# Where ScalarE's squares and VectorE's y1, E and V stand beside the y2 normalization

## The reference

```
q = x + x@Wq.T + bq ; k1, k2, v1, v2 likewise, 16 heads of 8
S1 = k1'v1/n ; S2 = k2'v2/n ; S12 = S1*S2        (8x8 per head)
out = q@S1*v2mean*g1 + rowsum(S12)*g2 + q@S2*v1mean*g3 + q@S12*g4
attn = layernorm(out)*ln_g + ln_b, then @ Wo.T + bo
x1  = layernorm(x + attn)
y2  = x1 + relu(x1@w1 + b1)@w2 + b2
y3  = layernorm(y2)*gamma + beta + x1
out = layernorm(y3)
```

## Time and profile before

| | |
|---|---|
| median of 3 runs | 218.47 us (216.88 to 219.51) |
| profiled execution, own time | 216.88 us |
| its span, first to last instruction | 215.1 us |
| PE busy | 195.6 us (91%) |
| DVE busy | 163.5 us (76%) |
| ACT busy | 127.5 us (59%) |
| POOL busy | 134.2 us (62%) |
| PE share of the chain that ended last | 54% |
| DVE, ACT shares of it | 18%, 13% |

### The profile page before, as it was taken

One profiled execution on the slowest core, in us unless ns is written; L12 is line 12 of the kernel. 1 busy time (PEld: TensorE's weight loads), 2 busy tenths in 40 slices (PEclk: granted clock), 3 DMA queues, 4 the chain that ended last, 5 costly groups with the idle time before them and its releaser, 6 DMA issues.

```text
span 215.1 us, 4255 instructions
## 1 busy us (share of the span) xinstructions
PE 195.6 (91%) x1380; PEld 177.9 (83%) x1380; DVE 163.5 (76%) x477; ACT 127.5 (59%) x383; POOL 134.2 (62%) x173
## 2 busy tenths in 40 slices
PE   7879999999998999899989999899989999899930
PEld 7768998997997889787979999798979998888630
DVE  0155845989868987989688886898697878896895
ACT  3122448455559585766576566947575557867571
POOL 8324650465896569675966489755967397776230
PEclk9999999999999999999999999999999999999995
DMA  5999700000010100110010001010011001011012
GB/s 157 103 292 287 188 0 5 2 0 5 0 49 0 52 2 3 49 50 0 0 52 34 16 3 49 0 53 0 0 52 52 0 0 52 0 50 49 2 50 98
DMA packets 12145, 9.98 MB, mean 46 GB/s; under 512 B 642, under 2 KB 9995, under 8 KB 12123
## 3 DMA queue, kind: packets, MB, share of 16 engines
q1 hardware_dynamic: 11082, 8.53, 12.8%
q0 software_dynamic: 320, 0.85, 2.6%
q10 hardware_dynamic: 720, 0.33, 0.6%
HBM read 5.51 MB, written 4.19 MB: 45 GB/s over the span
## 4 chain that ended last, share of the span: by engine, by line
PE 54%; DVE 18%; ACT 13%; issue 8%; DMA 3%; SPq 2%; DVEq 0%; ACTq 0%
PE down_ps L890 17%; PE up_ps L890 14%; PE prep_ps L890 12%; PE z_ps L890 7%; DVE st L689 5%; ACT res L571 5%; DMA vec_rows<-in_L_ffn_b 3%; PE turn_ps L1010 3%; DVE y2n L694 3%; DVE x1T_lo L826 3%; ACT hT L588 2%; ACT z_sq L549 2%; ACT x1T_hi L638 2%; DVE z_ps L788 2%; PE turn_ps L983 2%
## 5 line engine op out<-in xcount | busy, mean ns | idle before, releaser
L890 PE MATMUL down_ps<-w_sb,hT 128*128 128x128 f32 x496 | 61.1, 277 | 0.1
L890 PEld LDWEIGHTS down_ps<-w_sb,hT 128*128 128x128 f32 x496 | 58.4, 192 | 1.2 <-DVE y2n L694 0.4
L588 ACT ACTIVATE hT<-up_ps,cols 128x512 f32<-128x512 f32 x64 | 41.6, 682 | 3.7 <-PE up_ps L890 3.5
L503 POOL TENSOR_TENSOR x1b<-x,b_rows 128x512 f32<-128x512 f32 x16 | 20.6, 1287 | 19.1 <-DVE x L694 19.1
L890 PE MATMUL up_ps<-x1T_hi,w_hi 128*128 128x512 f32 x64 | 26.5, 414 | 4.1 <-ACT hT L588 4.1
L477 POOL TENSOR_TENSOR y2g<-y2n,gamma_rows 128x512 f32<-128x512 f32 x14 | 17.9, 1279 | 13.4 <-DVE y2n L694 13.4
L571 ACT ACTIVATE res<-y,nb,rstd 128x128 f32<-128x128 f32 x60 | 24.6, 483 | 2.1 <-POOL nb L465 2.1
L890 PE MATMUL up_ps<-x1T_lo,w_hi 128*128 128x512 f32 x64 | 25.5, 398 | 0.0
L890 PE MATMUL up_ps<-x1T_hi,w_lo 128*128 128x512 f32 x64 | 25.2, 395 | 0.0
L549 ACT ACTIVATE z_sq<-z_ps 128x128 f32<-128x128 f32 x64 | 16.9, 272 | 12.3 <-PE z_ps L890 12.3
L694 DVE TENSOR_SCALAR x<-z_ps,st,rstd 128x128 f32<-128x128 f32 x64 | 21.9, 404 | 0.6
(11 more groups left out here) (144 smaller groups left out, 426.1 us busy)
## 6 DMA issues: line engine op xcount, KB each, us to landing
X<-in_L_attn_x SPq DMA_DIRECT2D x8, 512.0 KB, 7.9
out<-res SPq DMA_DIRECT2D x15, 256.0 KB, 2.0
w_sb<-in_L_ffn_w POOLq DMA_DIRECT2D x2, 256.0 KB, 8.4
out<-res SPq DMA_DIRECT2D x2, 128.0 KB, 1.9
w_raw<-in_L_attn_Wv ACTq DMA_DIRECT2D x2, 64.0 KB, 2.7
w_raw<-in_L_attn_Wk SPq DMA_DIRECT2D x2, 64.0 KB, 4.2
bv_rows<-in_L_attn_bv ACTq DMA_DIRECT2D x2, 64.0 KB, 4.4
bo_rows<-in_L_attn_bo ACTq DMA_DIRECT2D x1, 64.0 KB, 4.5
```

The source lines that it names most:

```text
L503: pool.tensor_tensor(x1b2[(s + 1) % 2][:, :, :], x1[:, :, :], rows(b2_rows[:, :]), ALU.add).then_inc(x1b2_out, 1)
L588: act.activation(hT[:, k, :], up_ps[k % len(up_ps)][:, :], ACT.Relu, bias=cols[:, 5 + k:6 + k]).then_inc(relu_out, 1)
L890: return pe.matmul(o, lhsT, rhs, start=start, stop=stop)
```

## The change

On ScalarE `squares` is split into the squares and `std_z` (the root `std1`). In a step without a preparation all four squares and `std1` now stand ahead of `std3`. In preparation steps from 2 on, the first two squares stand ahead of `std3` and the other two and `std1` behind it. On VectorE, in steps from 0 on without a preparation (`y1_first`), `rstd1` and y1 stand ahead of `rstd3` and y2n, while y1's statistics stay where they were, behind `y3_stats`. In preparation steps E and V stand ahead of `rstd3` and y2n. No instruction is added or removed, and TensorE's, GpSimd's and SyncE's lists are untouched.

```diff
--- before.py
+++ after.py
@@ -540,14 +540,17 @@
 
                 act.activation(dst[:, :], src, ACT.Sqrt, bias=eps_col[:, :], scale=scale).then_inc(done, 1)
 
-            def squares(m):
+            def squares(m, tiles):
 
                 wait(act, r1_out, m)
-                for t in range(TILES):
+                for t in tiles:
                     if t % 2 == 0:
                         wait(act, z_done, m * 2 + (t // 2 + 1))
                     act.activation(z_sq[:, t, :], z_ps[t // 2][:, t % 2 * 256:t % 2 * 256 + C], ACT.Square,
                                    accum_out=z_sum[:, t:t + 1]).then_inc(sq_out, 1)
+
+            def std_z(m):
+
                 wait(act, sq_out, m * TILES + TILES)
                 std(z_sum[:, :], std1, std1_out, 1.0 / C)
 
@@ -595,12 +598,18 @@
                     xT_upper(0)
                     output_weights()
                     gram_out(1)
+                split = st.prep and st.n > 0
+                if st.nxt:
+                    squares(n + 1, range(2 if split else TILES))
+                    if not split:
+                        std_z(n + 1)
                 if st.prev:
 
                     wait(act, st3_out, n)
                     std(two(st3, 2), std3, std3_out, 1.0 / C)
-                if st.nxt:
-                    squares(n + 1)
+                if split:
+                    squares(n + 1, range(2, TILES))
+                    std_z(n + 1)
                 if st.cur:
                     if st.n == 0:
                         act.wait_ge(ffn_rows, FFN_ROWS)
@@ -738,15 +747,21 @@
                 dve.tensor_tensor(down_ps[:, :].rearrange("p (t c) -> p t c", c=C), down_ps[:, :].rearrange("p (t c) -> p t c", c=C),
                                   x1b2[s % 2][:, :, :], ALU.add).then_inc(y2_out, 1)
 
+            def sum_y1(n, s):
+
+                m = n + 1
+                wait(dve, std1_out, m + 1)
+                dve.reciprocal(rstd1[:, :], std1[:, :]).then_inc(r1_out, 1)
+                wait(dve, r1_out, m + 1)
+                wait(dve, xu_out, m + 1)
+                for t in range(TILES):
+                    last = dve.scalar_tensor_tensor(out=y1_tile(t), in0=y1_tile(t),
+                                                    scalar=rstd1[:, t:t + 1], in1=xu[(s + 1) % 2][:, t, :],
+                                                    op0=ALU.mult, op1=ALU.add)
+                last.then_inc(y1_out, 1)
+
             def body(st):
                 n, s = st.n, st.s
-                if st.prev:
-
-                    wait(dve, std3_out, n)
-                    dve.reciprocal(rstd3[:, :], std3[:, :]).then_inc(r3_out, 1)
-                    wait(dve, r3_out, n)
-                    wait(dve, y2g_out, n - 1)
-                    normalize(y2n, y2_tile, st3, rstd3, y2n_out)
                 if st.prep:
 
                     b = st.prepared()
@@ -765,6 +780,16 @@
                                       nbv_rows[:, :, :].rearrange("p j c -> p (j c)"), ALU.add).then_inc(EV_out, 1)
                 if st.n == -2:
                     factors()
+                y1_first = st.nxt and not st.prep and n >= 0
+                if y1_first:
+                    sum_y1(n, s)
+                if st.prev:
+
+                    wait(dve, std3_out, n)
+                    dve.reciprocal(rstd3[:, :], std3[:, :]).then_inc(r3_out, 1)
+                    wait(dve, r3_out, n)
+                    wait(dve, y2g_out, n - 1)
+                    normalize(y2n, y2_tile, st3, rstd3, y2n_out)
                 if st.prev2:
                     y3_stats(n - 2, s % 2)
                 if st.n == -1:
@@ -777,19 +802,11 @@
                     u_row()
                     xT_rest(0)
                     PQ_rest(0)
+                if st.nxt and not y1_first:
+                    sum_y1(n, s)
                 if st.nxt:
 
-                    m = n + 1
-                    wait(dve, std1_out, m + 1)
-                    dve.reciprocal(rstd1[:, :], std1[:, :]).then_inc(r1_out, 1)
-                    wait(dve, r1_out, m + 1)
-                    wait(dve, xu_out, m + 1)
-                    for t in range(TILES):
-                        last = dve.scalar_tensor_tensor(out=y1_tile(t), in0=y1_tile(t),
-                                                        scalar=rstd1[:, t:t + 1], in1=xu[(s + 1) % 2][:, t, :],
-                                                        op0=ALU.mult, op1=ALU.add)
-                    last.then_inc(y1_out, 1)
-                    wait(dve, y1_out, m + 1)
+                    wait(dve, y1_out, n + 2)
                     stats(y1_pairs, st2, st2_out)
                 if st.prev2:
                     result_factors(n - 2)
```

## The result

The changed kernel takes 223.68 us (median of 4 runs, 221.68 to 224.56), the kernel before 218.53 (216.88 to 219.51): 5.15 us or 2.4% more by the medians; the ratio of the runs is 1.0255 with an interval of 1.0198 to 1.0311. Forecast were 224.6 us and +6.15. Every ratio here is taken over the fast runs of both kernels and not from the medians printed beside it, so the two can differ by some tenths of a percent: a run over 1.5% above the fastest of its kernel counts as slow, and is left out of the ratio though not of the median and the range.

A forecast was written before the change was run, and what follows sets the result against it. TensorE was taken as close to the bound in steps 7 and 8, with VectorE's late x1 setting step 5's end. The terms summed to +6.15 us, against the median of 218.47 a forecast of 224.6 us, range 221.0 to 226.8.

The forecast's parts named there:

- steps 1 and 2: First steps: squares were not late, so y1 gains nothing and y2n runs after it; +0.82 us for the two.
- steps 3 to 6: Two pairs of steps, each +0.25 from later x1 and +0.12 on TensorE from later M_sb; +0.74 us.
- steps 7 to 12: Three pairs of steps, each +0.10 for an exposed weight load and +0.58 from later M_sb; +2.04 us.
- step 13: Step without preparation, with x1 later as in step 5; +0.25 us.
- step 14: std1 stays bound by z, y2n and y2g come later, and so does x1T_hi; +2.3 us, through x1 alone +1.5.
- The stall moves, it does not go: Step 5: the 0.6 to 0.75 us before up(5,3) go, but down matmuls wait for y2n, starting 90.63 instead of 90.65.
- GpSimd's thin cover: Step 5: GpSimd's work starts 1.6 us later, but xu and ScalarE's res still finish in time, by 0.1 and 0.4 us.
- rival 4: Costs more: GpSimd's cover fails, 0.3 more in each of steps 3 to 13, or TensorE's clock falls; 226.5 to 227; chance 0.11.
- S and M_sb: Preparation steps: S starts 2.89 us after E, making M_sb late; TensorE loses 0.58 in steps 8, 10, 12.
- Rival 1: Faster: the stall in front of up(n,3) is truly gained; with step 14 hidden as well 215.5 us; chance 0.04.
- Rivals 2 and 3: Preparation steps cost TensorE nothing, 221.5 us, chance 0.10; and step 14 is hidden, 222.4 us, chance 0.09.
- rival 2: Preparation steps: S's delay does not reach TensorE, early V gives some 0.2; 3.0 in all, 221.5 us; chance 0.10.

The follow-up runs named there:

- e1: The change's part for steps without preparation alone, preparation steps as in the kernel before: 221.03 against 216.89 us for the kernel before, ratio 1.0174.
- e5: Kernel before with only ScalarE's four squares and std1 ahead of std3 in steps without preparation, VectorE untouched: 223.36 against 217.63 us, ratio 1.0247.
- f2: Kernel before with, in steps 3 to 13 without preparation, four squares ahead of std3, std1 behind it, and y3_stats ahead of rstd3: 214.38 against 217.63 us.
- e2: The change's part for preparation steps alone, other steps as in the kernel before: 218.53 against 216.89 us for the kernel before, ratio 1.0061.
- e3: Changed kernel with step 14 put back as it was: 220.92 against 216.89 us for the kernel before, ratio 1.0175.
- e4: Changed kernel with GpSimd's mr and nb ahead of y2g in step 14 only: 222.09 against 216.89 us for the kernel before, ratio 1.0222.
- f3: f2 with rstd2 and x1 also ahead of xT_lo in the same steps: 213.36 against 217.63 us for the kernel before, ratio 0.9789.
- g1: Kernel before with seven unused matmuls added on TensorE in front of turn_vectors: 217.06 against 217.54 us, ratio 1.0013.
- g2: f3 with seven unused matmuls added on TensorE in front of turn_vectors: 211.84 against 217.54 us for the kernel before, ratio 0.9755.

## Why the prediction was right

The sign, the size and the places came out. Term by term, forecast and measured shift: steps 1 and 2 0.82 and 0.78; steps 3 to 6 0.74 and 0.61; steps 7 to 12 2.04 and 1.89; step 13 0.25 and 0.22; step 14 2.3 and 2.20; behind it 0 and 0.01. The sum is 6.15 against 5.7: the first five terms were high, by 0.03 to 0.15 each. The timed medians differ by 5.15 (2.4%); the ratio's interval of 2.0% to 3.1% takes in 5.7 (2.6%).

**The stall moves, it does not go.** Forecast was a start of the down matmuls where it had been, with a wait for y2n instead of relu; the profile has the wait. Step 5 begins 2.17 later than before (87.22 against 85.05); less that, `rstd1` stands at 87.75, y2n ends at 90.58 and the down matmuls start at 90.63, each as forecast. e1 gives +0.22 and +0.09 for the two kinds of step. e5 and f2, where y2n does not come last, show the down matmuls of step 5 starting 0.81 and 0.84 earlier, without a wait. The 0.25 itself was right for the reason given: 0.35 more idle time at the start, and 0.13 back, forecast 0.11, because y1's statistics no longer stand directly behind y1. From `rstd1` at 89.92 to the end of y1's statistics at 94.08 are 4.16 us, against 91.68 - 87.39 = 4.29 before. So of the Trainium skill's section "The DRAIN you can't avoid" ("VectorE: DVE Perf Modes") the addition, that an operation which is not held starts earlier, fits this trace, and the strict reading does not: `rstd3` at 91.17 starts 0.10 before the four y1 tiles end at 91.27.

**GpSimd's thin cover held.** In step 5 xu ended at 97.03, 0.15 before `x1b2`, and `res` at 97.58, 0.27 before `x1T_hi`, where 0.1 and 0.4 had been estimated; rival 4's loss in each of steps 3 to 13 did not come. Nor did its other half: the granted clock of the kernel after is 1.00 from 18 to 212 us, and TensorE's new idle time in step 14 is 1.06 us, not 1.3.

**S and M_sb.** The 2.89 from E to S measured 2.90, and TensorE's loss 0.54 to 0.55 where 0.58 was forecast. e2 shows the cost by itself. In steps 4 and 6 it is 0.08 and 0.09 where 0.12 was forecast. One sign was read too small: VectorE's idle time before E was to be about 0.5, and is 0.49 in steps 4 and 6 but 1.39 in steps 8, 10 and 12; the longer idle time adds nothing, since E starts at `gram_av`'s end either way. That V's earlier end is worth something in step 2 only e2 brought out (0.25 alone, 0.14 behind the longer step 1); for steps 1 and 2 together the forecast of 0.82 held.

**Steps 1 and 14.** e3 takes 2.2 us away, and e4 splits them into 0.7 for GpSimd and 1.5 for x1, as the forecast's +1.5 through x1 alone had it. That these two steps cost so much more than the 0.22 of step 5 has the reason given: there `std1` is bound by z and does not come earlier. Counted from the `x1T_hi` of the step before, it starts after 2.81 in step 1 (2.83 before) and 2.56 in step 14 (2.55 before), but after 2.37 in step 5 (3.37 before).

**The rivals.** Rival 1 (the stall in front of `up(n,3)` gained) was wrong for this edit because y2n was put behind y1; f2 shows the same gain as real, 0.7 in each of steps 7, 9 and 11, once VectorE's idle time takes what is moved. Rivals 2 and 3 are refuted by e2 and e3. Two of the rivals' sums do not come out of their terms: for rival 2, 6.15 less the preparation steps' 1.98 and V's 0.2 is 4.0 (222.4 us) and not 3.0, and for rival 4, 224.6 and 11 x 0.2 to 0.3 is 226.8 to 227.9, so that the range's upper end took in only its lower edge. The median forecast missed by 0.9 us; 0.45 of that is the sum, the rest lies within the runs' spread, of which the clock at the start is a part.

## What to carry to other kernels

Before an operation is moved ahead on a busy in-order engine, list what it is moved past and who waits for that: the time given to relu was taken from y2n, and TensorE waits for both. Look for work without a wait (here `y3_stats`) that fits an idle time already there, and put that in front; together with the squares' move it gained 3.5 us in steps 3 to 13, where the change with its exchange of waiting operations lost 2.7 in steps 3 to 13 and 5.7 in all. And look at each kind of step apart, the first and the last above all: where the data of what is moved ahead come no earlier (`std1` in steps 1 and 14) nothing is gained, and all that now stands behind it is late, 1.0 and 2.2 us here against 0.2 in step 5.

## What the hardware showed that was not expected

In 7 of the first 10 profiles (the kernel before, the changed one and eight others) TensorE's granted clock fell between 9 and 18 us, to means of 0.50 to 0.85 from 12 to 15 us, that is, between its levels of 1.2 and 2.4 GHz in part of the time, and was at 1.00 from 18 us on. It fell after TensorE had idled for the vectors' DMA (`vec_rows`), as the timelines of PE before and after have it:

```profile
11.46 0.22 PE L910 MATMUL z_ps<-ident,vec_rows 9*128 9x9 f32 x1 [1.73 <-DMA vec_rows<-in_L_ffn_b]
```

```profile
11.69 0.22 PE L927 MATMUL z_ps<-ident,vec_rows 9*128 9x9 f32 x1 [2.81 <-DMA vec_rows<-in_L_ffn_b]
```

This idle time was 1.89 to 2.81 us in the seven profiles in which the clock fell and 1.54 to 1.78 in the three in which it stayed at 1.00 (before, e2, f3); but with 1.44 us in g1, behind the seven added matmuls, it fell, and with 0.43 in g2 it stayed.

What it costs can be read off. From this matmul to the first `x1T_hi` are 18.34 or 18.35 us in the four profiles with the clock at 1.00, and 19.18 to 19.50 in the eight others: 0.8 to 1.2 us. The rest of what moves the first `x1T_hi`, between 28.98 and 31.40 us in the twelve profiles, is the start of the matmul itself, 10.48 to 12.22, which waits for the DMA. Of the 1.09 us between the kernel before and the changed one, 0.86 are thus the clock and 0.23 the DMA, and neither has to do with the change. Why the clock falls in some executions only is open; filling part of the idle time did not settle it.
